# A gated cross-attention and mixture-of-experts kernel on one core: residual kept in two x buffers, search rounds regrouped, low weight parts of the first stage through TensorE, masks in a buffer of their own

## The reference, cut to what matters

```python
# x (4, 512, 512), ctx_512 (4, 512, 128); _layernorm over the last axis
def xattn(h, adj_raw, Wq, Wk, gamma_raw):          # 4 heads
    sim = einsum('bhnd,bhmd->bnm', Q, K) / (sqrt(32) * 4)     # 512 x 512 per batch
    threshold = top_k(sim, 153)[0][:, :, -1:]
    A = sigmoid(sim) * (sim >= threshold)
    A = (A + swapaxes(A, -1, -2)) * 0.5
    return (1 - gamma) * adj_raw + gamma * A        # gamma = sigmoid(gamma_raw)
def ffn(x, ...):
    y, g = split(xf @ shared_gw.T, 2); shared = silu(g) * y @ shared_dw.T        # width 704
    scores = sigmoid(xf @ gate_w.T); two of eight experts per token, by scores + gate_bias
    out = sum over experts of (silu(g_e) * u_e) @ down_w[e].T * w_e              # width 352
    return shared + out
x = x + tanh(g_xattn) * xattn(ctx_512, _layernorm(x), Wq, Wk, gamma_raw)
x = x + tanh(g_ffn) * ffn(_layernorm(x), ...)
```

## Time and profile before

| | |
|---|---|
| median of 3 runs | 594.91 us (593.76 to 595.9) |
| the profiled execution | 595.18 us, span 593.4 us |
| mean granted TensorE clock | 0.925 of full |
| busy share: PE, DVE, ACT, POOL | 86%, 58%, 44%, 39% |
| opening (to the first logits) | 0 to 79.8 us |
| periods 0, 1, 2 (logits to logits) | 67.0, 62.1, 59.8 us |
| last batch and the expert tiles | from 268.7 us |

### The profile page before, as it was taken

The page is one execution under the profiler, slowest core; times in us unless marked ns, Lnnn a source line. Parts: engine busy times, 40 slices in busy tenths (PEclk is TensorE's granted clock), DMA queues, the critical chain, the costliest instruction groups (busy, mean ns, idle before and its releaser), DMA issues.

```text
span 593.4 us, 11085 instructions
## 1 busy us (share of the span) xinstructions
PE 507.4 (86%) x3169; PEld 289.1 (49%) x3170; DVE 343.6 (58%) x708; ACT 262.0 (44%) x473; POOL 232.2 (39%) x226
## 2 busy tenths in 40 slices
PE   2402589979998999879998899999999999999992
PEld 0100354434444454344464466666666666666660
DVE  0589758787868786977974377533333333333330
ACT  1696588646774579433231156322222222222221
POOL 1147735462446434550233034343343343443422
PEclk9655769989998999997999799999999999999997
DMA  3235293205611472034004489545445445445333
GB/s 113 97 91 173 80 305 108 57 30 182 250 42 36 138 275 57 21 106 147 1 1 159 149 230 242 123 77 95 79 75 95 78 78 96 74 77 97 74 43 46
DMA packets 32050, 63.75 MB, mean 107 GB/s; under 512 B 4049, under 2 KB 4305, under 8 KB 32017
## 3 DMA queue, kind: packets, MB, share of 16 engines
q1 hardware_dynamic: 23280, 42.89, 22.1%
q0 software_dynamic: 8736, 20.45, 18.9%
HBM read 41.05 MB, written 22.28 MB: 107 GB/s over the span
## 4 chain that ended last, share of the span: by engine, by line
PE 58%; DVE 17%; ACT 9%; issue 7%; DMA 5%; POOL 2%; SPq 1%; DVEq 1%; POOLq 0%; ACTq 0%
PE py L1004 12%; PE pg L984 12%; PE pu L985 12%; PE pg L845 4%; PE pu L845 4%; PE pt_bank L804 3%; DVE w L1178 3%; DVE pa L1137 3%; DVE w L1108 2%; PE pa L994 2%; PE py L862 2%; ACT w L613 2%; ACT w L619 2%; PE pu L862 2%; DVE w L1141 1%
## 5 line engine op out<-in xcount | busy, mean ns | idle before, releaser
L984 PE MATMUL pg<-w,x_t 128*128 x468 | 140.7, 313 | 0.0
L985 PE MATMUL pu<-w,x_t 128*128 x468 | 140.7, 313 | 0.0
L541 POOL DMA_INDIRECT out<-rows,idx x39 | 61.8, 1584 | 142.3 <-ACT rows L744 134.6
L1004 PE MATMUL py<-w,work 128*128 x351 | 82.1, 379 | 0.8 <-DVE work L1435 0.8
L845 PE MATMUL pg<-w 128*128 128x512 f16 (+1 forms) x288 | 80.2, 389 | 1.9 <-DVE work L1231 1.9
L845 PE MATMUL pu<-w 128*128 128x512 f16 (+1 forms) x288 | 79.7, 387 | 0.0
L734 ACT ACTIVATE work<-pg 128x352 f32<-128x352 f32 x39 | 18.0, 463 | 135.2 <-PE pu L985 135.2
L580 ACT ACTIVATE w<-stage 128x544 f16<-128x544 f32 (+1 forms) x80 | 50.7, 647 | 34.8 <-DMA stage<-in_weights 34.6
L488 POOL TENSOR_TENSOR w<-stage,w 128x544 f16<-128x544 f32 (+1 forms) x43 | 54.0, 1264 | 27.4 <-ACT stage L584 25.5
L494 POOL TENSOR_TENSOR work<-work 128x512 f16<-128x512 f32 (+1 forms) x24 | 29.0, 1209 | 81.9 <-ACT work L649 81.9
L1424 DVE SCALAR_TENSOR_TENSOR work<-pu,work 128x352 f32<-128x352 f32 x39 | 20.5, 524 | 62.6 <-ACT work L734 62.5
(11 more groups left out here) (189 smaller groups left out, 760.8 us busy)
## 6 DMA issues: line engine op xcount, KB each, us to landing
stage<-in_weights SPq DMA_DIRECT2D x80, 272.0 KB, 3.1
w<-in_x SPq DMA_DIRECT2D x4, 1024.0 KB, 6.6
out<-w SPq DMA_DIRECT2D x16, 256.0 KB, 2.8
xn_rows<-w SPq DMA_DIRECT2D x16, 256.0 KB, 5.3
out<-rows SPq DMA_DIRECT2D x13, 256.0 KB, 3.2
rows<-out SPq DMA_DIRECT2D x12, 256.0 KB, 3.0
w<-in_ctx_t SPq DMA_DIRECT2D x4, 256.0 KB, 3.4
out<-rows,idx POOLq DMA_INDIRECT x39, 4.7
```

What stands on the lines that cost most here:

```text
L541: pool.indirect_dma_start(out=out, out_offset=bass.IndirectOffsetOnAxis(ap=idx[:, t:t + 1], axis=0), in_=rows[:, t % 2, :], in_offset=None ...
L984: pe.matmul(pg[p][:, 0:H], lhs, w[:, item, half, at:at + H], start=begin, stop=end)
L985: mm = pe.matmul(pu[p][:, 0:H], lhs, w[:, item, half, at + H:at + 2 * H], start=begin, stop=end)
L1004: mm = pe.matmul(py[:, :], hid_t[:, p, part * JC + j, :], w[:, item, half, at:at + C], start=(j, part, half) == (0, 0, 0), stop=(j, part) ...
```

## The change

**Residual.** There are two x buffers `xbs` (one beside the weights, where item 6 goes later), used in turn. The residual of a batch stays in its buffer, takes the shared network's result there and is stored once; the stores of `store_attended` and the loads of `reload` are gone. The x of batch b + 2 is loaded when batch b is stored.

**Masks.** They are written to `kept` (now L1172), no longer over `att`; `check` (did a row miss its threshold) stands apart from `masks`, later in the order. VectorE does x * gain + kept (L1217) and adds the turned matrix and the shift (L1224). ScalarE's `base` and GpSimd's `add_attention` are gone. ScalarE writes the normalised rows once, in float16 (L612), and VectorE computes them again in float32 (`exact`, L1235) for the low part.

**Search.** In a period, rounds 0 and 1 stand before the first unit's product, rounds 2 and 3 before the second's; thresholds, masks and the statistics of x follow. GpSimd's `base_scalars` now stands behind the fourth unit.

**Weights.** The opening takes 12 pieces, each period 12 (SLOT_PIECES says how many behind each unit). The low parts of pieces 0 to 7 are made by TensorE as 256 * stage - high (`low_pieces`) and taken from its banks by ScalarE (`low_from_banks`). TensorE waits in period 0 for pieces as it needs them (`pieces_ready`). `shared_down` runs tile by tile, and the loops over the periods are written out.

```diff
-BEFORE = 3
-FIRST = 14
-BY_DVE = 20
+BY_PE = 8
+FIRST = 12
+PER_PERIOD = 12
+SLOT_PIECES = (0, 1, 2, 2, 2, 2)
...
-        xb = attn_tiles()
+        beside = w[:, EARLY - 1, :, :].rearrange("p b c -> p (b c)").bitcast(F32)
+        xbs = [beside[:, 0:TPB * SEQ].rearrange("p (i c) -> p i c", i=TPB), attn_tiles()]
+        kept = beside[:, TPB * SEQ:2 * TPB * SEQ].rearrange("p (i c) -> p i c", i=TPB)
         sim = attn_tiles()
...
+        def by_pe(item, n):
+            return item * CHUNKS + n < BY_PE
+
+        def low_pair(k):
+            return k % 2 if k < BY_PE - 2 else 0
+
...
+        def period_pieces(b):
+            k = FIRST + b * PER_PERIOD
+            slots = []
+            for count in SLOT_PIECES:
+                slots.append([(j // CHUNKS, j % CHUNKS) for j in range(k, k + count)])
+                k += count
+            rest = [(j // CHUNKS, j % CHUNKS) for j in range(k, FIRST + (b + 1) * PER_PERIOD)]
...
+            base_scalars(0)
             guess(0)
-            base_scalars(0)
-            def first_pieces(begin, end):
-                for k in range(begin, end):
-                    low_piece(k // CHUNKS, k % CHUNKS)
-
-            first_pieces(0, FIRST)
-            add_attention(0)
...
+            after(pool, a_made, 1)
+            low_piece(1, 0)
+            row_scalars(0, 0)
+            row_scalars(0, 1)
+            for n in range(1, FIRST - CHUNKS):
+                low_piece(1, n)
             guess(1)
             o.clear()
...
             def together(b, more):
-                base_scalars(b + 1)
+                slots, rest = period_pieces(b)
                 for u in range(UPS):
                     shared_low(b, u)
-                    if u < TPB:
-                        low_piece(b + BEFORE, u)
-                add_attention(b + 1)
-                for n in range(TPB, CHUNKS - 2):
-                    low_piece(b + BEFORE, n)
-                row_scalars(b + 1)
-                for n in range(CHUNKS - 2, CHUNKS):
-                    low_piece(b + BEFORE, n)
+                    if u == TPB - 1:
+                        base_scalars(b + 1)
+                    for piece in slots[u]:
+                        low_piece(*piece)
+                for piece in rest:
+                    low_piece(*piece)
+                row_scalars(b + 1, 0)
+                row_scalars(b + 1, 1)
...
+            def low_from_banks(k):
+                at = k % CHUNKS * CHUNK_W
+                for half in range(2):
+                    after(act, low_mm, k * 2 + half + 1)
+                    act.activation(w[:, k // CHUNKS, 1, at + half * HALF_W:at + (half + 1) * HALF_W],
+                                   low_banks[low_pair(k)][half][:, 0:HALF_W], ACT.Copy).then_inc(w_lo[k % RING] if half else low_sb, 1)
...
+            high_piece(0, 3)
+            low_from_banks(2)
+            high_piece(0, 4)
+            low_from_banks(3)
+            high_piece(0, 5)
+            low_from_banks(4)
+            keep_qk(1)
+            low_from_banks(5)
+            high_piece(0, 6)
+            high_piece(0, 7)
+            low_from_banks(6)
+            low_from_banks(7)
+            for n in range(FIRST - CHUNKS):
+                high_piece(1, n)
+            scores_and_rows(0, True)
...
                 for u in range(UPS):
                     shared_silu(b, u)
...
+                    if u == 0:
+                        count(b + 1, 2)
+                    if u in (1, 2):
+                        scaled_sigmoid(b + 1, 2 * u - 2)
+                        scaled_sigmoid(b + 1, 2 * u - 1)
+                    shared_high(b, u)
+                    if u == 0:
+                        count(b + 1, 3)
+                    for piece in slots[u]:
+                        high_piece(*piece)
+                for piece in rest:
+                    high_piece(*piece)
...
+            def low_pieces(begin, end):
+                for k in range(begin, end):
+                    at = k % CHUNKS * CHUNK_W
+                    after(pe, w_hi, k + 1)
+                    for half in range(2):
+                        bank_, lo, hi = low_banks[low_pair(k)][half], half * HALF_W, (half + 1) * HALF_W
+                        if low_uses(k):
+                            last = low_uses(k)[-1]
+                            after(pe, w_lo[last % RING], last // RING + 1) if half else after(pe, low_sb, last + 1)
+                        pe.matmul(bank_[:, 0:HALF_W], scaled_ident[:], stage[:, k % RING, lo:hi], start=True, stop=False)
+                        pe.matmul(bank_[:, 0:HALF_W], minus_ident[:], w[:, k // CHUNKS, 0, at + lo:at + hi],
+                                  start=False, stop=True).then_inc(low_mm, 1)
+
+            def pieces_ready(n):
+                for r_, s in enumerate(w_lo):
+                    after(pe, s, len(range(r_, n, RING)))
+                after(pe, w_hi, n)
...
+                if b == 0 and 0 in ks and off == 0:
+                    pieces_ready(half * CHUNKS + -(-UP_W // CHUNK_W) if half else BY_PE)
...
+                if b == 0 and 0 in pieces and i == 0:
+                    pieces_ready(HALVES * CHUNKS)
...
+            low_pieces(0, 4)
             missed_rows(0)
             project(1, None)
+            low_pieces(4, 6)
+            after(pe, w_lo[5 % RING], 5 // RING + 1)
             turn_attention(0)
             for i in range(TPB):
                 scores(1, i)
+            low_pieces(6, 8)
             for i in range(TPB):
...
                 logits(b)
                 for u in range(UPS):
                     shared_up(b, u, b + 1)
-                shared_down(b, 0, range(0, 4))
                 missed_rows(b + 1)
-                shared_down(b, 1, range(0, 4))
-                shared_down(b, 0, range(4, UPS))
-                shared_down(b, 1, range(4, UPS))
+                shared_down(b, 0)
                 turn_attention(b + 1)
                 if more:
                     project(b + 2, b)
-                shared_down(b, 2)
+                shared_down(b, 1)
                 if more:
...
+            x_stats(0)
             score_stats(0, range(TPB))
...
+            masks(0)
+            check(0)
...
+                search(b + 1, 0)
+                search(b + 1, 1)
+                shared_hidden(b, 0)
+                search(b + 1, 2)
+                search(b + 1, 3)
+                shared_hidden(b, 1)
+                thresholds(b + 1, (0, 1))
+                shared_hidden(b, 2)
+                thresholds(b + 1, (2, 3))
+                count_missed()
+                shared_hidden(b, 3)
+                masks(b + 1)
                 x_stats(b + 1)
```

More of the change, by code:

```diff
@@ L253, in scaled_pieces @@
         def scaled_pieces(item, n):
[L254 to L259, removed]
+            return item * CHUNKS + n + 1 - BY_PE
+        ROWS_DVE = BATCHES * (TPB // 2)
         Q0 = BATCHES * UPS
@@ L668, in _ @@
             keep_scores(0)
+            for n in range(ROUNDS):
+                count(0, n)
+            high_piece(0, 0)
+            high_piece(0, 1)
+            low_from_banks(0)
             score_tanh(0)
+            high_piece(0, 2)
+            low_from_banks(1)
             act.wait_ge(cst_ok, 1)
@@ L1077, in low_piece, with statistics @@
                                          op0=ALU.mult, op1=ALU.subtract).then_inc(w_lo[n % RING], 1)
-            def statistics(s):
+            def statistics(s, tiles=range(TPB)):
                 o.wait()
-                for i in range(TPB):
+                for i in tiles:
                     o.mark(dve.bn_aggr(mv[:, s, i, :], bn6[:, s, i, :]))
@@ L1175, in masks @@
                         f.then(dve.tensor_copy(thr[:, i:i + 1], top8[:, i, (KEEP - 1) % 8:(KEEP - 1) % 8 + 1]))
-                after(dve, sig_sb, (b + 1) * TPB)
-                for i in range(TPB):
-                    dve.scalar_tensor_tensor(out=att[:, i, :], in0=sim[:, i, :], scalar=thr[:, i:i + 1], in1=att[:, i, :],
-                                             op0=ALU.is_ge, op1=ALU.mult).then_inc(a_made, 1)
+                        f.then(keep(b, i))
+                o.wait()
+                dve.sem_inc(a_made, 1)
             def attended(b, more, shared):
@@ L1184, in x1_stats @@
                     after(dve, x1_made, b * TPB + i + 1)
-                    o.mark(dve.bn_stats(bn6[:, 2, i, :], xb[:, i, :]))
+                    o.mark(dve.bn_stats(bn6[:, 2, i, :], xbs[b % 2][:, i, :]))
+                    if i % 2:
+                        statistics(2, (i - 1, i))
+                        dve.sem_inc(ln_stats, 1)
+                after(dve, base_ok, b + 1)
+                for i in range(TPB):
+                    o.mark(dve.scalar_tensor_tensor(out=xbs[b % 2][:, i, :], in0=xbs[b % 2][:, i, :], scalar=pt[:, 4, i:i + 1],
+                                                    in1=kept[:, i, :], op0=ALU.mult, op1=ALU.add))
                 if shared is not None:
```

379 lines of the change are left out of this document (158 added, 221 removed).

## The result

The changed kernel takes **607.16 us** (median of 4 runs, 606.79 to 607.61), the kernel before 594.35 in the same runs: ratio 1.0212, 95% interval 1.0189 to 1.0234. It is slower by 12.8 us; forecast were 2.6 more, in a range that ended at 605.

What follows compares the result with a forecast made beforehand. TensorE, busy 86% of the span, was taken as the bound, with 24 us of waits and slow clock in the periods. Terms 0 + 3.5 + 1.8 - 0.9 - 2.0 = +2.4 gave 597.5 us, range 588.5 to 605.

Steps and rivals of the forecast that it cites:

- The opening's term of 0: Opening: earlier attention addition lost again on GpSimd, logits at 79.7, units at 81.1; 0 us, ends -2 and +3.
- The wait ahead of the fourth unit: Period 0: TensorE stands 5.2 us for piece 13, held in ScalarE's and GpSimd's queues.
- period 0: First period: wait for piece 13, slow clock and the row tile's wait; +3.5 us, ends -2 and +6.
- period 1: Second period: 63.9 us instead of 62.1, with the row tile's wait and slow clock; +1.8, ends -2.5 and +4.
- period 2: Third period: 58.9 us instead of 59.8, with the same row-tile wait; -0.9, ends -4 and +2.
- last batch and behind it: Last batch: without a gap before it, first products can run at 2.4 GHz; -2.0 us, ends -2.4 and 0.
- The wait that replaces the one for the masks: Periods' first row tile: TensorE waits for GpSimd's low parts behind base_scalars, 4.9 us; the 2.46 us mask wait goes.
- They end at 29.9 to 31.5, I take 30.7: Periods 1 and 2: when VectorE's statistics of x end, in us from the period's first logits.
- 30.8 + 2.6 + 6 x 1.2 = 40.6: GpSimd, periods 1 and 2: base_scalars' start, its chain, then four pieces and two low parts; sixth low part ends.
- 1.5 (slow clock behind two waits ...): Periods 1 and 2: 1.5 us for TensorE's slow clock behind two waits of 1.8 and 3.0 us.
- All that follows has room: Periods, behind the row tile: GpSimd's pieces end at 47.5, scalars at 49.3 and 51.1, turned rows needed at 56.
- Rival B: Whole kernel: masks stretched by contention delay the statistics 1.5 us a period, 0.7 more clock; 604 (601 to 608), chance 0.20.

Runs made afterwards that it cites:

- run 9: Run 5 with GpSimd's weight pieces last, plus opening turned: GpSimd's row scalars before its first piece, ScalarE's normalised rows before pieces 8 to 11; 594.93 us.
- Run 10: Run 2's kernel with no weight pieces in the third slot (1, 1, 0, 2, 2, 2), four behind the last unit; 601.31 us.
- Run 7: Changed kernel with products that nothing reads put into TensorE's two row-tile waits in periods 1 and 2; 605.30 us.
- Run 2: Changed kernel with weight pieces dealt 1, 1, 2, 2, 2, 2 instead of 0, 1, 2, 2, 2, 2, so piece 13 comes one unit earlier; 604.74 us.
- run 1: Changed kernel with GpSimd's base_scalars moved behind the sixth unit's low part instead of the fourth's; 617.81 us.
- run 3: Changed kernel with the edits of run 1 and Run 2, and VectorE's statistics of the next x behind the fifth unit's product; 604.71 us.
- run 4: Changed kernel with TensorE taking four units of both first row tiles, then the last two units of both, as in the kernel before; 616.06 us.
- run 5: Changed kernel with VectorE's order statistics, fifth product, masks, sixth product, and pieces dealt 1, 1, 2, 1, 1, 2; 594.05 us.
- run 6: Changed kernel with GpSimd making the low weight pieces of the second and third units' slots twice; 613.88 us.

## Why the prediction was wrong

**Right.** The opening's term of 0: logits at 79.51, units at 80.95, forecast 79.7 and 81.1, and for the reason given (the scalars behind the low part of piece 8 at 66.29; run 9 takes it away). The wait ahead of the fourth unit was 6.99, forecast 5.2. The wait that takes the masks' place is GpSimd's L480 in the first row tile, `base_scalars` idle before it for VectorE's statistics; no wait for masks is left. Only period 0 has less of it than forecast (1.39 where "3 us or more" was to be the longest in each period).

The terms, forecast and measured in the profiled executions:

| | forecast | measured |
|---|---|---|
| opening | 0 | -0.3 |
| period 0 | +3.5 | +6.5 |
| period 1 | +1.8 | +7.6 |
| period 2 | -0.9 | +3.8 |
| last batch and behind it | -2.0 | -5.7 |

**The step that failed** is "The wait that replaces the one for the masks": its place was right, its terms were too small. For period 1, relative to its logits (153.06):
- "They end at 29.9 to 31.5, I take 30.7": 33.5. Thresholds took 5.9 and 5.4 us, not 4.4: GpSimd's operations stood beside both pairs of subtractions (1.66 and 1.41 each, 0.65 where it is silent), in the kernel before beside one, 4.4 against 3.9. Run 10 took one piece away from the second pair and got 1.0 us back.
- "30.8 + 2.6 + 6 x 1.2 = 40.6": the sixth low part ended at 45.0. Of these 4.4 us, 2.8 come from the statistics, 0.3 from the chain of `base_scalars`, and 1.3 because two pieces took 3.28 and the low part 1.59 beside VectorE's additions. The waits were 4.93 + 3.36 = 8.3, forecast 4.9: +3.4.
- "1.5 (slow clock behind two waits ...)": turning and projection took 5.95 us (199.44 to 205.39), forecast 1.9 + 1.7, and the row tile 13.7, of which 5.4 without its waits, forecast 3.9. Slow clock so took 3.9 us instead of 1.5: +2.4. Run 7, which kept the clock at 1.00, gives 3.0 back.

Together 69.7 against 63.9; period 2 repeats it (63.6 against 58.9). Period 0 took 73.5 against 70.5; 1.8 of the 3.0 are the wait for piece 13. Run 2 shows that 4.2 us less of this wait give only 2.4, since the row tile then waits longer.

**"All that follows has room"** held in the changed kernel: from the first addition to the last turned rows VectorE took 29.8 us in period 1, 6.8 of them waiting. But the room is no larger than that. Without waits VectorE needs 23 us, and runs 1, 3 and 4 lost there what they won. The additions that GpSimd made before (L468) are in this chain as L1217, 5.6 to 5.8 us for four beside GpSimd's pieces, 2.74 without (52.85, in the opening).

**The last batch** gave -5.7 us, forecast -2.0, and made the total look better than the periods were. I had counted the 6.5 us at half clock of the earlier trace rows. The windows of the kernel before from its last logits:

```profile
268.75:282.00 13.25, 12.70 (x105) 6.34 (x104) 8.90 (x31) 4.81 (x7) 0.00 (x0) 0.76 0.42 144
282.00:332.00 50.00, 46.87 (x244) 25.93 (x242) 33.61 (x77) 11.00 (x19) 12.69 (x10) 0.94 0.22 70
```

and of the changed kernel:

```profile
286.42:300.00 13.58, 13.56 (x118) 7.29 (x119) 10.30 (x37) 5.58 (x9) 0.00 (x0) 1.00 0.30 104
300.00:350.00 50.00, 46.68 (x264) 26.76 (x263) 33.97 (x73) 9.94 (x18) 12.74 (x11) 1.00 0.26 87
```

13.25 us at 0.76 and 50 at 0.94 are 3.2 and 3.0 us of clock (estimate), now none: a third of the 17.9 us lost in the periods was hidden so. Why the clock held there was not tested; run 7 lost 3.6 us in the same stretch.

Rival B (contention and clock, 604) was nearest, with its mechanism in the thresholds and not in the masks, which took 0.91 each (1.39 in the earlier trace rows).

## What to carry to other kernels

Before filling or shortening a wait, look for the second chain that ends at the same time; here the edits that eased or filled the row tile's waits and left or delayed VectorE's start (runs 1, 3, 4, 7) won at most 2.5 us over the changed kernel or lost 9 to 11, and run 5, in which both chains start earlier, won 13. Cost a two-operand operation by what will stand beside it after the change, not by the row of before.

## What the runs showed of the hardware

VectorE's subtraction with two 128x512 operands took 0.65 us alone and 1.41 to 1.66 beside GpSimd's subtractions, while counts (0.74) and MAX8 (0.68) kept their length; GpSimd's own took up to 1.6 instead of 1.2. So the price was 0.8 to 1.0 us, most of GpSimd's whole operation. The Trainium skill, *SBUF — State Buffer*, section "SBUF: two separate sides", says why, for VectorE operations with two SBUF inputs or in a two-port mode: the port pair that the two share is locked for a full instruction, and who comes second is blocked. The trace agrees with that rule. The one-operand row of 1.14 us (0.15 alone) in run 6 ends at 181.83, as GpSimd's pieces do (181.81), and two one-operand rows of 128x512 (L1235) took 2.68 us in the opening beside GpSimd's pieces, 1.00 in the periods without: not only operations with two inputs meet it. Which of these run in a two-port mode no trace shows.

Behind waits of 4.93 and 3.36 us TensorE's granted clock was 0.50 (1.2 GHz) for 5 us; where the waits held products (run 7) and 1.0 to 1.5 us of each was left, it was 1.00 (2.4 GHz) throughout both periods.
